# An integer-quantised attention and feed-forward kernel: scalars through another queue, one weight maximum on another engine, and a new issue order where stage two begins

## What is computed

```python
def fake_quant(x, s, z):                       # 8-bit, zero point z
    return (clip(round(x / s + z), 0, 255) - z) * s

x = x + fake_quant(layernorm(x)) @ fake_quant(ctx)            # x: 2 x 1024 x 2048, ctx: 2 x 2048 x 2048

h = bf16(layernorm(x))                                        # 2048 rows of 2048
qg, sg = dynamic_quant(h * inv_gate)                          # int8 rows, one scale per row
qu, su = dynamic_quant(h * inv_up)
inter = bf16(clip(silu(qg @ w_gate.T * sg * s_wgate) * (qu @ w_up.T * su * s_wup), -10, 10))
qi, si = dynamic_quant(inter * inv_inter)                     # rows of 1024
x = x + qi @ w_down.T * si * s_wdown                          # w_gate, w_up: 1024 x 2048; w_down: 2048 x 1024
```

## Time and profile before

| | |
|---|---|
| median of 3 runs (us) | 1009.84 |
| lowest and highest (us) | 1008.09, 1012.61 |
| the profiled execution's own time (us) | 1010.6 |
| its span from first to last instruction (us) | 1008.9 |
| granted clock of TensorE, mean | 0.979 |
| busy: TensorE, VectorE, ScalarE, GpSimd (us) | 926.1, 691.4, 362.1, 243.7 |
| DMA, mean over the span | 176 GB/s |

### The profile page before, as it was taken

The page is one execution under the profiler, slowest core; times in us unless marked ns, Lnnn a source line. Parts: engine busy times, 40 slices in busy tenths (PEclk is TensorE's granted clock), DMA queues, the critical chain, the costliest instruction groups (busy, mean ns, idle before and its releaser), DMA issues.

```text
span 1008.9 us, 11458 instructions
## 1 busy us (share of the span) xinstructions
PE 926.1 (92%) x4304; PEld 418.6 (41%) x4304; DVE 691.4 (69%) x1018; ACT 362.1 (36%) x281; POOL 243.7 (24%) x240
## 2 busy tenths in 40 slices
PE   1688889999996749999999999999999999999998
PEld 0333344444442314444444444444444444444443
DVE  4579356438499678899888887777747795444444
ACT  3836358556455652333333323232326510000000
POOL 2317746354446001233333121222200000000000
PEclk9799999999998989999999999999999999999999
DMA  9666697974959703244333333333269722973222
GB/s 357 266 248 233 214 365 271 338 271 113 366 223 346 223 21 95 78 102 103 95 95 94 94 79 89 94 84 81 46 192 298 276 100 76 351 272 136 84 84 83
DMA packets 123367, 177.43 MB, mean 176 GB/s; under 512 B 102704, under 2 KB 102704, under 8 KB 105648
## 3 DMA queue, kind: packets, MB, share of 16 engines
q1 hardware_dynamic: 118528, 142.62, 44.5%
q10 hardware_dynamic: 4752, 34.08, 8.7%
q0 software_dynamic: 32, 0.00, 0.1%
HBM read 113.77 MB, written 37.75 MB: 150 GB/s over the span
## 4 chain that ended last, share of the span: by engine, by line
PE 72%; DVE 9%; DMA 8%; issue 5%; ACT 3%; POOL 2%; SPq 1%; ACTq 0%; DVEq 0%; POOLq 0%
PE ps L1106 40%; PE ps L1118 22%; PE ps L1086 8%; DMA ctx_stage<-in_ctx 4%; DVE w_slots L834 2%; DMA q1T<-x_q 2%; PE ps L1055 1%; DMA x_scratch<-x_tile 1%; DVE small_operands L774 1%; DVE ctx_u L747 1%; DMA w_raw<-in_w_gu 1%; DVE small_operands L865 1%; SPq L267 1%; ACT x_q L467 1%; ACT x_i L459 1%
## 5 line engine op out<-in xcount | busy, mean ns | idle before, releaser
L1106 PE MATMUL ps<-w_slots,qT_even 128*128 128x512 f16 x1024 | 226.2, 383 | 23.1 <-DVE w_slots L834 15.9
L1086 PE MATMUL ps<-ctx_slot,q1T 128*128 128x512 f16 x1024 | 232.6, 388 | 13.4 <-DVE q1T L754 6.1
L1106 PE MATMUL ps<-w_slots,qT_odd 128*128 128x512 f16 x1024 | 224.5, 381 | 9.2 <-issue 9.2
L1118 PE MATMUL ps<-w_slots,qiT 128*128 128x512 f16 x1024 | 221.2, 379 | 0.0
L1106 PEld LDWEIGHTS ps<-w_slots,qT_even 128*128 128x128 f16 x1024 | 100.8, 99 | 147.0 <-DVE w_slots L834 16.4
L1086 PEld LDWEIGHTS ps<-ctx_slot,q1T 128*128 128x128 f16 x1024 | 101.0, 100 | 139.8 <-issue 8.4
L1106 PEld LDWEIGHTS ps<-w_slots,qT_odd 128*128 128x128 f16 x1024 | 100.1, 98 | 132.1 <-issue 12.9
L1118 PEld LDWEIGHTS ps<-w_slots,qiT 128*128 128x128 f16 x1024 | 100.2, 98 | 120.8
L526 ACT ACTIVATE q_f<-q_i 128x2048 f16<-128x2048 int8 x32 | 61.1, 1910 | 155.8 <-DVE q_i L846 155.4
L915 DVE SCALAR_TENSOR_TENSOR down_tmp<-ps,small_operands,down_scales_b 128x512 f32<-128x512 f32 x64 | 47.9, 749 | 92.2 <-PE ps L1118 92.2
L679 POOL TENSOR_TENSOR x_tile<-x_tile,col_bias 128x512 f32<-128x512 f32 x64 | 98.1, 1554 | 39.0 <-DVE x_tile L793 39.0
(11 more groups left out here) (93 smaller groups left out, 699.3 us busy)
## 6 DMA issues: line engine op xcount, KB each, us to landing
ctx_stage<-in_ctx ACTq DMA_DIRECT2D x32, 1024.0 KB, 8.4
x_scratch<-x_tile SPq DMA_DIRECT2D x16, 1024.0 KB, 6.2
w_raw<-in_w_gu SPq DMA_DIRECT2D x16, 1024.0 KB, 8.7
x_tile<-x_scratch SPq DMA_DIRECT2D x16, 1024.0 KB, 8.4
x_tile<-in_x SPq DMA_DIRECT2D x15, 1024.0 KB, 8.7
x_and_xs<-x_scratch SPq DMA_DIRECT2D x15, 1024.0 KB, 5.0
out_x<-x_tile SPq DMA_DIRECT2D x15, 1024.0 KB, 5.1
w_raw<-in_w_dn SPq DMA_DIRECT2D x8, 1024.0 KB, 9.8
```

Source lines behind the costliest of these rows:

```text
L1086: last = nc.tensor.matmul(ps[:, bank(g), :], q1T[m][:, k, :], ctx_s[j % 4][:, k, :], start=(k == 0), stop=(k == KT - 1))
L1106: last = nc.tensor.matmul(ps[:, bank(S2 + i), :], qT[t % 2][:, which, k, :], wsl[:, unit(p, k // 4), hl, k % 4, :], start=(k == 0 and hl = ...
L1118: last = nc.tensor.matmul(ps[:, bank(S3 + i), :], qiT[t % 8][:, k, :], wsl[:, unit(4 + c, k // 4), hl, k % 4, :], start=(k == 0 and hl == ...
```

## The change

There are three edits.

1. The load of the quantisation scalars moves from GpSimd's queue to SyncE's, behind the first half of tile 0. On VectorE the statistics of tile 0 move ahead of the ten small steps and the clearing of buffers.
2. The fourth granule of part 3 gets its maximum on VectorE: a new function `w_max`, one reduction with absolute value over 128 x 2048. ScalarE keeps the other three; the counts of `abs_done` behind it are one lower.
3. The order around the first products of stage two changes. ScalarE takes the first maximum of part 3 ahead of the second conversion of tile 1, converts part 2 in one go, takes two more maxima and converts part 3 with one `silu` inside. VectorE subtracts part 2 in one go, then `w_max`, `w_scale(3)`, and part 3 in two pairs around `evac_up(1, 0)`; `ln2_stats(2)` comes behind all of it. On SyncE's queue the first transposition of tile 0 goes ahead of the loads of part 2, tile 15 is stored before tile 14, and the load of granule (3,3) goes behind the second transposition of tile 1.

```diff
@@ SyncE
+            load_x(0)
+            sp.dma_start(qp[:, :], params.partition_broadcast(P)).then_inc(params_in, 16)
-            for m in range(8):
+            for m in range(1, 8):
                 load_x(m)
...
             load_x2(1)
+            transpose_q(0, 0)
             sp.wait_ge(pe_done, chunk_end[6])
             load_w(2, 0)
             load_w(2, 1)
-            transpose_q(0, 0)
             sp.wait_ge(pe_done, chunk_end[7])
             load_w(2, 2)
             load_w(2, 3)
             transpose_q(1, 0)
-            for m in (13, 14, 15):
-                store_x2(m)
+            store_x2(13)
+            store_x2(15)
             load_w(3, 0)
             transpose_q(0, 1)
-            for g, m in ((1, 15), (2, 13), (3, 14)):
+            store_x2(14)
+            for g, m in ((1, 15), (2, 13)):
                 sp.wait_ge(x2_stored[m % 8], 32)
                 load_w(3, g)
             transpose_q(1, 1)
+            sp.wait_ge(x2_stored[14 % 8], 32)
+            load_w(3, 3)
             load_x2(2)
-            sp.wait_ge(abs_done, 16)
+            sp.wait_ge(abs_done, 15)
@@ ScalarE
             silu(0, 0)
+            w_abs(3, 0)
             cast_q(1, 1)
-            w_hi(2, 0)
-            w_hi(2, 1)
+            for g in range(4):
+                w_hi(2, g)
+            w_abs(3, 1)
+            w_abs(3, 2)
+            w_hi(3, 0)
             silu(1, 0)
-            w_hi(2, 2)
-            w_hi(2, 3)
-            for g in range(4):
-                w_abs(3, g)
-            w_hi(3, 0)
-            w_hi(3, 1)
+            for g in range(1, 4):
+                w_hi(3, g)
             h_bf16(2)
             silu(0, 1)
-            w_hi(3, 2)
-            w_hi(3, 3)
@@ GpSimd
-            pool.dma_start(qp[:, :], params.partition_broadcast(P)).then_inc(params_in, 16)
@@ VectorE
+            def w_max():
+                dve.wait_ge(w_loaded[15], 16)
+                dve.wait_ge(wmax_ready, 2)
+                nc.vector.tensor_reduce(wsum[:, 7:8], raw[:, raw_unit(3, 3), :], AX.X, ALU.max,
+                                        apply_absolute_value=True).then_inc(last_max, 1)
...
             def w_scale(p):
                 power = wsc[:, p:p + 1]
-                dve.wait_ge(abs_done, part_granules(p))
+                dve.wait_ge(abs_done, part_granules(p) - (p >= 3))
+                if p == 3:
+                    dve.wait_ge(last_max, 1)
...
+            ln1_stats(0)
+            dve.wait_ge(params_in, 16)
+            nc.vector.tensor_scalar(d12[:, 0:1], qp[:, 1:2], -1.0, CENTRE, ALU.mult, ALU.add)
...
             for buffer in (tcol, trow, tback):
                 nc.vector.memset(buffer, 0.0)
-            ln1_stats(0)
             quant_quad(0)
...
             evac_up(0, 0)
-            w_lo(2, 0)
-            w_lo(2, 1)
+            for g in range(4):
+                w_lo(2, g)
+            w_max()
+            w_scale(3)
             evac_gate(1, 0)
-            w_lo(2, 2)
-            w_lo(2, 3)
-            w_scale(3)
-            evac_up(1, 0)
             w_lo(3, 0)
             w_lo(3, 1)
+            evac_up(1, 0)
+            w_lo(3, 2)
+            w_lo(3, 3)
             ln2_stats(2)
             sw_scale(2)
             evac_gate(0, 1)
-            w_lo(3, 2)
-            w_lo(3, 3)
             sw_scale(3)
```

More of the change, by code:

```diff
@@ L136, in build @@
         w_loaded = [sem(f"w_loaded{i}") for i in range(24)]
-        abs_done, wmax_ready = sem("abs_done"), sem("wmax_ready")
+        abs_done, last_max, wmax_ready = sem("abs_done"), sem("last_max"), sem("wmax_ready")
         scale_step, wsc_ready, hi_done, lo_done = sem("scale_step"), sem("wsc_ready"), sem("hi_done"), sem("lo_done")
@@ L477, in w_abs @@
                 n = granule_no(p, g)
+                summed = n - (n > 15)
                 act.wait_ge(w_loaded[n], 16)
@@ L486, in w_abs @@
                     act.wait_ge(xs_ready[1], NT)
-                if n:
-                    act.wait_ge(abs_done, n)
+                if summed:
+                    act.wait_ge(abs_done, summed)
                 junk = junk_early if n < 8 else junk_late if n < 16 else junk_down
@@ L721, in link @@
                 dve.wait_ge(semaphore, count[0])
-            dve.wait_ge(params_in, 16)
-            nc.vector.tensor_scalar(d12[:, 0:1], qp[:, 1:2], -1.0, CENTRE, ALU.mult, ALU.add)
-            nc.vector.tensor_scalar(d12[:, 1:2], qp[:, 3:4], -1.0, CENTRE, ALU.mult, ALU.add)
-            nc.vector.tensor_scalar(z1c, qp[:, 1:2], -CENTRE, None, ALU.add)
-            nc.vector.reciprocal(is1, qp[:, 0:1])
-            nc.vector.reciprocal(is2, qp[:, 2:3])
-            link(nc.vector.tensor_tensor(s12, qp[:, 0:1], qp[:, 2:3], ALU.mult), setup, n_setup)
-            nc.vector.tensor_tensor(cbs, s12, d12[:, 0:1], ALU.mult)
-            link(nc.vector.tensor_tensor(rta, s12, d12[:, 1:2], ALU.mult), setup, n_setup)
-            link(nc.vector.tensor_scalar(rtb, cbs, d12[:, 1:2], float(D), ALU.mult, ALU.mult), setup, n_setup)
-            nc.vector.tensor_copy(rterm[:, 0:1], rtb).then_inc(scalars_ready, 1)
             def cast_done(q):
@@ L921, in down @@
                                                ALU.add, ALU.add).then_inc(res_done, 1)
+            ln1_stats(0)
+            dve.wait_ge(params_in, 16)
+            nc.vector.tensor_scalar(d12[:, 0:1], qp[:, 1:2], -1.0, CENTRE, ALU.mult, ALU.add)
+            nc.vector.tensor_scalar(d12[:, 1:2], qp[:, 3:4], -1.0, CENTRE, ALU.mult, ALU.add)
+            nc.vector.tensor_scalar(z1c, qp[:, 1:2], -CENTRE, None, ALU.add)
+            nc.vector.reciprocal(is1, qp[:, 0:1])
+            nc.vector.reciprocal(is2, qp[:, 2:3])
+            link(nc.vector.tensor_tensor(s12, qp[:, 0:1], qp[:, 2:3], ALU.mult), setup, n_setup)
+            nc.vector.tensor_tensor(cbs, s12, d12[:, 0:1], ALU.mult)
+            link(nc.vector.tensor_tensor(rta, s12, d12[:, 1:2], ALU.mult), setup, n_setup)
+            link(nc.vector.tensor_scalar(rtb, cbs, d12[:, 1:2], float(D), ALU.mult, ALU.mult), setup, n_setup)
+            nc.vector.tensor_copy(rterm[:, 0:1], rtb).then_inc(scalars_ready, 1)
             for buffer in (tcol, trow, tback):
                 nc.vector.memset(buffer, 0.0)
-            ln1_stats(0)
             quant_quad(0)
```

## The result

The changed kernel takes 999.21 us (median of four runs, 997.77 to 1000.1). The kernel before, on the same chip, takes 1011.23 us (four runs, 1008.09 to 1012.82). The ratio is 0.9883, with a 95% interval of 0.9864 to 0.9902: the change makes the kernel 1.2% faster, some 12 us. The profiled execution took 997.77 us, 12.8 us less than the one before (1010.6), and 1.4 us less than its own median.

What follows compares the result with a forecast made beforehand. TensorE was taken as the bound where it is busy throughout, with gains only before (3,0), at the start and stage two's entry: 1010.6 - 3.1 - 7.3 = 1000.2 us, 999.4 beside the median, range 996 to 1004.5.

Steps and rivals of the forecast that it cites:

- The likeliest of the cases: Gains of 3.1 us at the start and 7.3 us in stage two both hold: 999.4 us, chance 0.62.
- the first term: Kernel start, edit 1: ScalarE begins tile 1 3.1 us earlier, and that reaches the end; bounds 0 and 3.8.
- the second: Entry into stage two, edits 2 and 3: tile 2's chain, and with it product (3,0), comes 7.3 us earlier.
- the times that were named as signs: Trace times that would show it right, among them `smooth_gate` of tile 2 near 369 and (3,0) near 413.7.
- The start: ScalarE begins tile 0 at 12 to 13.8 us, tile 1 near 21.1, as the second quad's landing does not move.
- 3.1 us pass through stage one: Stage one: transfers follow engine progress, so the start's 3.1 us arrive whole; rival that they are caught, 1002.5 us, chance 0.15.
- Part 3: Part 3 of the weights, entry into stage two: last subtraction ends at 365.4 instead of 379.1, 13.7 us earlier.
- The rival that made this landing 3.4 or 10.8 us late: Granule (3,3)'s load: 3.4 us late gives 1002.8, chance 0.10; 10.8 us late gives 1010.2, chance 0.04.
- Tile 2's chain: Stage two: tile 2's copy usable at about 372.1 instead of 379.40, so (2,1) and (3,0) come 7.3 us earlier.
- The branch stays long: Tile 2's second branch: VectorE's product beside GpSimd again takes 2.05 us; if short, 1.4 us more won at most.
- The clock: Stage two, TensorE: (2,1) starts slow after a wait, (3,0) at 417.3 instead of 416.8, time 999.9; chance 0.05.
- The queue: SyncE's queue: tile 0's first transposition ahead of part 2's loads starts TensorE's first product earlier, but gains zero.

Runs made afterwards that it cites:

- the statistics alone: Kernel before with only tile 0's statistics moved ahead of VectorE's ten small steps, scalars still on GpSimd's queue; 1008.46 us.
- the start alone: Kernel before with only edit 1 (scalars' load on SyncE's queue, tile 0's statistics ahead of the ten steps); 1007.15 us, ratio 0.9962.
- stage two alone: Changed kernel with edit 1 undone, so only edits 2 and 3 remain; 1002.85 us, ratio 0.9917 to the kernel before.
- the transposition back: Changed kernel with tile 0's first transposition again behind part 2's first two loads on SyncE's queue; run twice, 1001.72 us (0.9906) and 999.77 us (0.989).
- the run with earlier statistics: Changed kernel with tile 2's statistics right behind part 3's power of two, its copy and two rescalings reordered on ScalarE; 997.95 us (0.9866), again 998.38 us (0.9875).
- the maximum back on ScalarE: Changed kernel with the maximum of part 3's fourth granule on ScalarE again instead of VectorE; 1001.18 us, ratio 0.9903 to the kernel before.

## Why the prediction was right, point by point

**The total.** Predicted 999.4 us (996 to 1004.5), measured 999.21. The likeliest of the cases held. That the two agree to 0.2 us is luck: the predicted gain was 10.4 us from a median of 1009.84, the measured one is 12.0 us from 1011.23, and the two differences cancel. In the profiled executions the first term is 2.6 us larger than predicted and the second 0.3 us smaller (5.7 and 7.0 for 3.1 and 7.3). By the excess of the first, the times that were named as signs came 2.4 to 2.5 us sooner than forecast: `smooth_gate` of tile 2 at 366.50 for 369, (3,0) at 411.33 for 413.7.

**The start.** Predicted: tile 0 at 12 to 13.8, tile 1 near 21.1. Measured: 12.23 and 21.00. The working was right in its main point: the second quad's landing hardly moves, and it catches 1.1 of 4.37 us. Two misses cancel in it. The scalars landed at 8.93, between the bounds of 5.8 and 9.6 and near the upper one, though the lower was taken; as the statistics take VectorE until 8.52 in any case, that cost 0.43 us. GpSimd's factors were taken at 3.02 us and took 2.1. The run with the statistics alone says which half does the work.

**3.1 us pass through stage one.** In size this is the step that missed. Stage one ended 5.7 us earlier in the profiled execution, not 3.1. Over the nine traces with tile 0's statistics in front (eight with the whole of edit 1) it ended between 297.95 and 303.45, with a median of 299.24; the three others (one with the scalars' queue changed) have 302.75 to 303.67. So the gain at that point is typically 4.4 us against before's 303.67, and anything from 0.2 to 5.7. The timed runs of the start alone, 3.8 us (2.5 to 5.1), hold both 3.1 and 4.4.

Where the other 2.6 us arose can be read from TensorE. Up to the group of twenty matmuls near 72 us the gain is 3.06 us (it starts at 71.54 where it was 74.60), as predicted. Two places add to it. In the trace of before:

```profile
120.31 19.17 PE L1086 MATMUL ps<-ctx_slot,q1T 128*128 128x512 f16 x88 [2.77 <-DMA q1T<-x_q]
...
155.54 1.07 PE L1066 MATMUL ps<-identity,x_q 128*128 128x128 f16 x16 [2.48 <-ACT x_q L467]
156.44 8.76 PE L1086 MATMUL ps<-ctx_slot,q1T 128*128 128x512 f16 x32
```

And in the changed kernel:

```profile
115.97 19.17 PE L1095 MATMUL ps<-ctx_slot,q1T 128*128 128x512 f16 x88 [0.79 <-DMA q1T<-x_q]
...
151.02 1.07 PE L1075 MATMUL ps<-identity,x_q 128*128 128x128 f16 x16 [1.11 <-ACT x_q L472]
151.93 7.07 PE L1095 MATMUL ps<-ctx_slot,q1T 128*128 128x512 f16 x32
```

The first is a wait for a tile transposed by DMA: the group behind it starts 4.34 us earlier, 1.3 us more. The second are 32 matmuls that took 8.76 us, at a granted clock of 0.56 (a mean, mostly 1.2 GHz) in the first 3.6 us, behind a wait of 2.48 us one step earlier. They take 7.07 us at 1.00 (2.4 GHz), where that wait is 1.11 us, and the next step starts 5.90 us earlier (165.03 to 159.13). So the gain does not pass through stage one unchanged, as the prediction had it: a wait and a clock spell inside it came out differently. The slow version of that product occurs in all three traces with the statistics in their old place and in three of the nine with them in front, so it is no fixed part of the gain. Why the transposition is late in one execution and not in another stays open.

**Part 3.** Predicted: the last subtraction 13.7 us earlier in the time of its own stage. Product (0,3), which waits for it in both kernels, moved from 379.14 to 360.09, by 19.05; less the 5.72 us of stage one this is 13.3. The rest, 0.4, is the wait for granule (3,3): it landed 6.3 us behind its issue and not 5.3, at 340.58, and VectorE waited 0.40 us for it. An idle time of VectorE ahead of the maximum that a weight load ends was named as a sign of being wrong; it is there, in this small size. In the other six traces with the maximum on VectorE it does not occur. The rival that made this landing 3.4 or 10.8 us late did not occur, though the place was as tight as the working had it.

**Tile 2's chain.** Predicted 7.3 us. `smooth_gate` of tile 2 moved from 379.40 to 366.50, by 12.9, less 5.72: 7.2. Product (2,1) moved from 402.19 to 389.27, also 7.2; (3,0) by 7.0. The run of stage two alone has 7.7 there. From stage one's end to (3,0) the four traces with the old order of stage two have 120.4, 121.7, 121.8 and 122.1 us; the five with the new one (the change twice, stage two alone, and the transposition back twice) have 112.7 to 114.2. So the term is 7.9 us between their means (121.5 and 113.6), and a single trace is good to some 1.5 us. This is the term that carries the prediction, and its shape was right too: of 14.6 us taken from the wait ahead of (0,3), half comes back at (2,0), as 5.16 us of wait and 2.25 us of a slow product in place of more wait, because the statistics of tile 2 now stand behind the subtractions.

**The branch stays long.** The product beside GpSimd's instruction was taken to be long again, and took 4.09 us where it had taken 2.05. GpSimd's instruction in the trace of before:

```profile
385.92 4.10 POOL L672 TENSOR_TENSOR x_and_xs<-h_bf,inv_up_b 128x2048 f32<-128x2048 bf16 x1 [16.01 <-DVE q_i L846]
```

Now the product starts 0.54 us into GpSimd's 4.09 us and ends 0.54 behind it; before it started 2.60 us into the 4.10 and ended 0.55 behind. The Trainium skill, page SBUF — State Buffer, section Who interferes with whom, calls the pair of ports that the two engines share an exclusive lock. Both these rows and the 0.69 us in the run with earlier statistics agree with it. In both kernels the branch's row maximum, which needs GpSimd's result anyway, follows 0.91 us behind GpSimd's end. So the 1.4 us that the prediction kept as a possible gain was at most 0.9.

**The clock.** The rival put the slow start at (2,1); it fell on (2,0) instead. That product follows a wait of 5.16 us and took 9.32 us, with a granted clock of 0.50 (1.2 GHz) from 379.3 to 382.6. Product (0,3), behind a wait of 1.32 us, took 7.08 us at 1.00 (2.4 GHz), and the three products from 389.27, behind 0.70 us, 20.88 us as before. The slow one cost nothing: at full rate it would have ended at 386.3, and (2,1) had to wait for its tile until 389.27. The Trainium skill, page TensorE: Matmul & The Clock Gate, section What's actually happening, says that throttled is the default and activity releases it. The long waits here agree (3.43, 4.40 and 5.16 us: 8.75, 9.26 and 9.32 us), but a wait does not always bring it back: the two short ones did not. Nor is its length enough to tell: in other runs a wait of 3.39 us (the maximum back on ScalarE, first product) and one of 3.67 us (the transposition back, second run, third product) were followed by products of 7.07 us at 1.00.

**The queue.** Counted at zero, measured as zero where the two ran together (999.77 against 999.89 us).

## What to carry to other kernels

When a long wait is shortened, cost the next chain on the same engine before booking the gain: here half of 14.6 us came back one product later, and the price that counted was that of tile 2's chain. Read the gain at the last wait of the bounding engine, and split it at a point upstream that the edit does not touch; here the time between the two points agreed within 1.7 us over the traces of one order, where the times up to the first point differed by 5.5. Work that needs nothing from a load goes ahead of the wait for it on the engine's list; which queue issues the load of 2 KB was worth 0.6 us alone and 0.4 us behind that order (tile 1 from 21.41 to 21.00), no more than the spread of tile 1 over the eight traces of one start (20.68 to 21.26).

## What was not expected

One program ends stage one at quite different times. The kernel with the transposition turned back ended it at 303.45 us in one profiled execution and at 299.21 in the next, with tile 1 begun at 21.26 and 21.20. The edit stands behind stage one, so it is no cause of that. One thing that differs is which engine is held up where VectorE and GpSimd start within 0.1 us of each other near 71 us. In the slower of the two executions it was GpSimd:

```profile
71.03 1.34 DVE L738 TENSOR_SCALAR ctx_u<-ctx_stage,small_operands 128x2048 uint8<-128x2048 f32 x1
71.11 3.02 POOL L689 TENSOR_SCALAR ctx_slot<-ctx_u 128x2048 f16<-128x2048 uint8 x1 [23.34 <-ACT ctx_u L448]
...
74.18 6.18 PE L1095 MATMUL ps<-ctx_slot,q1T 128*128 128x512 f16 x20 [2.40 <-POOL ctx_slot L689]
```

In the other it was VectorE:

```profile
70.90 3.03 DVE L738 TENSOR_SCALAR ctx_u<-ctx_stage,small_operands 128x2048 uint8<-128x2048 f32 x1
70.94 1.90 POOL L689 TENSOR_SCALAR ctx_slot<-ctx_u 128x2048 f16<-128x2048 uint8 x1 [23.30 <-ACT ctx_u L448]
...
72.90 4.49 PE L1095 MATMUL ps<-ctx_slot,q1T 128*128 128x512 f16 x20 [1.25 <-POOL ctx_slot L689]
```

One of the two takes about 3 us, the other 1.3 to 1.9. VectorE starts first by the record in both, so starts that lie 0.04 to 0.08 us apart do not tell which. TensorE waits for GpSimd's cast, so with GpSimd held up it waits 2.40 us instead of 1.25, and the same twenty matmuls then take 6.18 us instead of 4.49. That is 2.84 us between the two traces.

But this does not decide the end of stage one. TensorE makes most of it good: its group of 64 matmuls starts at 103.07 in the slower execution and 102.58 in the other, 0.49 us apart. It falls back by 2.9 us at the wait for the transposed tile (120.23 and 117.35, behind 2.90 and 0.80 us), and by another 1.4 where 32 matmuls take 8.76 us instead of 7.07, the two places of the account above. Of the twelve traces only this one has GpSimd held up, while the kernel before, with the cast at 2.00 us, ends stage one at 303.67 all the same. Whether the late cast made that transposition late is not shown.
